# q, k and v products of an adaLN transformer block as split single passes, with q rows in three half sets and the work around them shifted

## The chip, the cores and the metric

The kernel runs on one core of a Trainium2 chip. The metric is the device time of one execution in microseconds (us), the median of several; the profile shows one execution of it. A second number, the span, is the time from the first to the last instruction of the profiled execution.

## The reference

For 32 batches of 512 tokens with 256 features, one transformer block with adaptive layer norm:

```python
mod = silu(c) @ wmod                       # per batch: sa, ca, ga, sb, cb, gb
h = layernorm(x) * (1 + ca) + sa
q, k, v = heads(h @ Wq + bq), heads(h @ Wk + bk), heads(h @ Wv + bv)   # 16 heads of 16
scores = (q / 4) @ k.T + 8 * position_bias[bucket(distance)]
x = x + ga * (softmax(scores) @ v @ Wo + bo)
h = layernorm(x) * (1 + cb) + sb
x = x + gb * fp4_linear(silu(fp4_linear(h, w_gate)) * fp4_linear(h, w_up), w_down)
```

`fp4_linear` rounds both operands, in blocks of 16, to a grid of FP4 values times a scale. The rounding makes the result sensitive to small errors ahead of it, which is why the kernel keeps its products near float32.

## The kernel before, in words

The program is written out for 36 iterations, n from -2 to 33, each of 16 slots s (0 to 15) of four places j (0 to 3). A place is written (s, j). Every engine walks through the same (s, j) in order, and semaphores tie them together; no scheduler moves anything. Three things run side by side in an iteration:

- **Attention of batch n.** In slot s the function `scores` writes two heads' scores for one block of 128 keys into a pair of PSUM banks, twice a slot (j = 0 and j = 2): a bf16 product over 121 rows (L630) and two or three small float16 products that add the band of the position bias (L633). ScalarE takes the exponential of each pair (L819); the pair's banks are free for the next `scores` only then. `weigh` at (s, 1) multiplies the probabilities of the slot before with the values (L665, float32).
- **Row maxima of the next batch.** At each (s, j) the function `maxima` (L647) makes one 128x512 tile of scores in one of two further banks, and VectorE (`reduce_max`, L1071 and L1073) adds the band and takes the maximum. The product of one place waits until the reduction of two places before has ended. The maxima of head h are made in slot h + 2. The jobs m0 and m1 turn the maxima of eight heads into rows that the scores product reads.
- **Jobs.** `job_table` gives each (s, j) zero or more jobs of TensorE, in three PSUM banks by turns: xT0, xT1 (transposes of normalised x), p0 to p3 (q and k products of batch n + 2, 256x256 times 256x512, a half of the heads each), v0 to v2 (v products), and the work on the token tiles, of which one tile per four slots passes through ctxT, wo, xqT, g0, g1, g2 (gate and up), oT, hT0, hT1 and down.

q and k are float32, and each is cut into three bf16 parts: ScalarE writes the product twice (`proj` in float32, part 0, L892), GpSimd subtracts part 0 (`rest`, L1287), ScalarE copies part 1 (L854), GpSimd subtracts again (`low`, L1294). The parts go to DRAM (L537), and `replicate` (L517) reads them back, six transfers for q and six for k of eight heads, into 96 rows of `q_rows` and `k_rows`, two buffers each of all 16 heads. The products p and v themselves are plain float32 matmuls of `h_t` (L704, L711), each of which the profile shows as two records. The products of the token tiles (`product`, L676) cut both operands into a high and a low float32r part instead and run three single passes: high times high, high times low, low times high.

In slots with s % 4 = 3 VectorE has the block scales of the hidden layer (L1108, L1110, L1112), on which GpSimd's multiply (L1357) waits, and on this ScalarE's square (L847) at (s, 3). At (s, 3) with s % 4 = 2 and (s, 0) after it VectorE subtracts the high part of the hidden transposes (`hq_l`, L1126), behind ScalarE's copies (L933, L936).

Iterations -2 and -1 hold only the start: setup of tables (`mod_and_bias_tables`, `spread_band`), the scales of the weights (`weight_scales`), q, k, v and maxima of batch 0.

Of the kernel before, what the change touches and what calls it, by code (L numbers as in the profile page):

```python
# [32 lines left out]
P = 128  # L33
# [9 lines left out]
HALF = 64  # L43
# [103 lines left out]
REST_AT, MID_AT, LOW_AT = (8, 9, 12, 13), ((8, 3), (9, 2), (12, 3), (13, 2)), (9, 10, 13, 14)  # L147
# [110 lines left out]
def build(nc, x, wq, wk, wv, wo, bq, bk, bv, bo, rel, wg, wu, wd, c_t, wmod, cst, rows_dram, band_dram, parts_dram, out):  # L258
    with ExitStack() as ctx:
# [7 lines left out]
        q_rows = [sb(f"q_rows{i}", [P, H, S], BF16) for i in range(2)]  # L267
# [4 lines left out]
        h_t = sb("h_t", [P, DT, S])  # L272
# [10 lines left out]
        w_q, w_k, w_v = (sb(n, [P, DT, D]) for n in ("w_q", "w_k", "w_v"))  # L283
# [8 lines left out]
        rev = sb("rev", [P, 3, P], F16)  # L292
# [5 lines left out]
        wait_pad = sb("wait_pad", [P, 1 + H * NT])  # L298
# [49 lines left out]
        a_act = Steps(sem("a_act"), "xh0 xh1 h0a h0b xh2 xh3 h1a h1b p0 hi0 p1 hi1 p2 hi2 p3 hi3")  # L348
# [42 lines left out]
        csb = flat(q_rows[1])  # L391
# [57 lines left out]
        def _(sp):  # L449
# [10 lines left out]
            for dst, src in ((w_q[:], wq), (w_k[:], wk), (w_v[:], wv)):  # L460
                load(dst, src.rearrange("(t p) n -> p t n", p=P), qkv_loaded)
# [9 lines left out]

            sp.wait_ge(su_act, SA["ind"])
            sp.dma_start(q_rows[0][CR], ind[CR].unsqueeze(1).broadcast_to([P - ROWS_QK, H, S])).then_inc(consts_placed, 16)
            sp.wait_ge(su_act, SA["band"])
            sp.dma_start(band_dram, band_sb).then_inc(band_stored, 16)
            sp.wait_ge(band_stored, 16)
            sp.wait_ge(su_pe, SP_["mod"])
            vec = band_dram
            for half in range(2):
                sp.dma_start(hank1[HALF * half:HALF * (half + 1)],  # L480
                             bass.AP(vec.tensor, vec.offset, [[1, HALF], [S, H], [1, 2 * P]])).then_inc(band_loaded, 16)
            sp.dma_start(hank2, bass.AP(vec.tensor, vec.offset,
                                        [[1, P], [S, H], [1, 3 * HALF]])).then_inc(band_loaded, 16)
# [24 lines left out]
            def replicate(it, half, back):  # L508

                n, par = it.n - back, (it.par + back) % 2  # L510

                wait(sp, scores_ready, 64 * n + 32 * (half + 1))
                for op, dst in ((0, q_rows[par]), (1, k_rows[par])):
                    wait(sp, parts_stored[2 * half + op], 16 * it.n + 16 * (3 - back))
                    src = parts_dram[par, half, op].rearrange("(h d) c n -> c d h n", d=HD)
                    for term, part in enumerate((TERMS_Q, TERMS_K)[op]):
                        sp.dma_start(dst[16 * term:16 * term + 16, 8 * half:8 * half + 8, :],  # L517
                                     src[part]).then_inc(replicated[half], 16)

            def emit(whole):  # L520
                it = whole
                n, par = it.n, it.par
                for s in range(16):
# [8 lines left out]
                    if s in (10, 14) and it.has(2):  # L532
                        for p in ((0, 1) if s == 10 else (2, 3)):
                            after(sp, low_pool, 4 * (n + 2) + p, "low")

                            wait(sp, replicated[p // 2], 16 * N_REP * (n + 1))
                            sp.dma_start(parts_dram[par, p // 2, p % 2], parts[:, p % 2]).then_inc(parts_stored[p], 16)  # L537
                    if s == 11 and it.has(2):
                        replicate(it, 0, 0)
# [29 lines left out]
        def _(pe):  # L569
# [23 lines left out]
            pe.wait_ge(qkv_loaded, 80)  # L593
# [806 lines left out]
```

## Time and profile before

| | before |
|---|---|
| runs | 3263.61, 3264.70, 3267.48 us; median 3264.7 |
| profiled execution | 3262.75 us, of which span 3260.9 us |
| busy, TensorE | 3137.3 us, 96% |
| busy, VectorE | 2765.6 us, 85% |
| busy, ScalarE | 2088.3 us, 64% |
| busy, GpSimd | 1732.0 us, 53% |
| mean granted TensorE clock | 0.982 of 2.4 GHz |

Busy times are unions of records. A matmul's record is longer than the time it holds the array, since the next starts before it ends; so the cost of a matmul is read from start to start. The same holds on VectorE and ScalarE, whose next instruction starts some 0.1 us before the end of the record in front.

### The profile page before, as it was taken

What the parts mean: (1) busy time and instruction counts of PE and PEld (TensorE: products, weight loads), DVE (VectorE), ACT (ScalarE), POOL (GpSimd) and SP (SyncE); (2) the same over time, 40 slices, a digit from 0 to 9 for tenths busy, and PEclk for the clock granted to TensorE, in tenths of its full rate; (3) what the DMA queues carried; (4) which work ended last, traced back from release to release, by engine and by line L of the source; (5) the groups of instructions that cost most, each with busy time, mean ns of one, the idle gap of its engine ahead of it and who ended that gap; (6) DMA issues with size and microseconds to landing.
All of it is one profiled execution on the core that took longest, in us unless ns stands there. A gap on an engine that the chain in (4) does not pass through costs nothing.

```text
span 3260.9 us, 67878 instructions
## 1 busy us (share of the span) xinstructions
PE 3137.3 (96%) x22404; PEld 1876.7 (58%) x22404; DVE 2765.6 (85%) x9960; ACT 2088.3 (64%) x3389; POOL 1732.0 (53%) x2104
## 2 busy tenths in 40 slices
PE   4899999999999999999999999999999999999985
PEld 1345566666656566665566665666666565666555
DVE  6678888888888888888888888888888888888865
ACT  2566666666666666666666666666666666666652
POOL 3415555555555555555555555555555555555455
PEclk7899999999999999999999999999999999999997
DMA  8344433334443324444233444332344433244000
GB/s 208 66 79 82 84 75 59 63 70 84 84 87 67 60 59 79 87 84 85 55 66 63 84 87 84 75 59 65 70 84 84 87 66 59 61 79 80 23 22 13
DMA packets 200187, 238.39 MB, mean 73 GB/s; under 512 B 23600, under 2 KB 178640, under 8 KB 199808
## 3 DMA queue, kind: packets, MB, share of 16 engines
q1 hardware_dynamic: 199840, 234.06, 37.1%
q8 instruction: 182, 2.98, 0.4%
q14 instruction: 165, 1.35, 0.2%
HBM read 164.57 MB, written 67.31 MB: 71 GB/s over the span
## 4 chain that ended last, share of the span: by engine, by line
PE 90%; issue 4%; DVE 3%; ACT 2%; DMA 1%; POOL 1%; SPq 0%; POOLq 0%; DVEq 0%; ACTq 0%
PE ps_x L676 25%; PE ps_o L665 15%; PE rings L647 14%; PE rings L630 14%; PE ps_x L704 6%; PE rings L633 5%; PE ps_x L711 3%; PE ps_x L722 2%; PE ps_x L743 2%; PE ps_x L735 1%; PE ps_x L728 1%; PE ps_x L697 1%; ACT probs L819 1%; DMA probs<-band_dram 0%; DVE row_max L1073 0%
## 5 line engine op out<-in xcount | busy, mean ns | idle before, releaser
L1073 DVE CUSTOM_DVE_ANT_0 rings<-rings,band_z 128x512 f32<-128x512 f32 x2048 | 1415.6, 696 | 70.5 <-issue 66.3
L819 ACT ACTIVATE probs<-rings 128x1024 f32<-128x1024 f32 x1024 | 1050.2, 1026 | 587.7 <-PE rings L633 587.5
L647 PE MATMUL rings<-k_rows,q_rows 120*128 120x512 bf16 x2048 | 790.6, 387 | 27.1 <-DVE row_max L1073 25.2
L630 PE MATMUL rings<-q_rows,k_rows 121*128 121x512 bf16 x2048 | 702.3, 383 | 12.3 <-ACT probs L819 11.2
L633 PEld LDWEIGHTS rings<-rev,band_t 128*128 128x128 f16 x5632 | 409.6, 98 | 299.9 <-issue 0.8
L665 PE MATMUL ps_o<-probs,values 128*32 128x512 f32 x4096 | 545.6, 605 | 0.0
L633 PE MATMUL rings<-rev,band_t 128*128 128x64 f16 x5632 | 500.6, 192 | 0.0
L647 PEld LDWEIGHTS rings<-k_rows,q_rows 120*128 120x128 bf16 x2048 | 197.4, 96 | 503.7 <-DVE row_max L1073 371.9
L1357 POOL TENSOR_TENSOR hidden<-hidden,inv 128x704 f32<-128x704 f32 x128 | 178.3, 1393 | 452.2 <-DVE inv L1112 452.2
L676 PE MATMUL ps_x<-w_gu_h,xq_h 128*128 128x512 f32 (+1 forms) x768 | 356.9, 465 | 1.1 <-DVE xq_l L1118 1.1
L1172 DVE SCALAR_TENSOR_TENSOR tanh<-tanh,ps_x 128x256 f32<-128x256 f32 (+1 forms) x384 | 152.3, 397 | 169.6 <-ACT tanh L929 165.3
L1073 DVE DVE_READ_ACCUMULATOR2_ANT row_max<- 128x1 f32 x2048 | 289.1, 141 | 0.0
L676 PE MATMUL ps_x<-w_gu_h,xq_l 128*128 128x512 f32 (+1 forms) x768 | 289.0, 376 | 0.0
L676 PE MATMUL ps_x<-w_gu_l,xq_h 128*128 128x512 f32 (+1 forms) x768 | 285.7, 372 | 0.0
L676 PE MATMUL ps_x<-w_dn_h,hq_h 128*128 128x256 f32 x768 | 240.6, 313 | 18.2 <-DVE hq_l L1126 18.2
L630 PEld LDWEIGHTS rings<-q_rows,k_rows 121*128 121x128 bf16 x2048 | 198.5, 97 | 92.7 <-issue 42.0
L1351 POOL TENSOR_TENSOR ffn_in<-ffn_in,inv 128x256 f32<-128x256 f32 x128 | 79.4, 620 | 303.8 <-DVE inv L1112 303.8
L1328 POOL TENSOR_TENSOR hidden<-hidden,magic 128x704 f32<-128x704 f32 x128 | 200.1, 1563 | 39.4 <-ACT magic L850 38.3
L676 PE MATMUL ps_x<-w_dn_l,hq_h 128*128 128x256 f32 x768 | 219.0, 285 | 0.0
L676 PE MATMUL ps_x<-w_dn_h,hq_l 128*128 128x256 f32 x768 | 218.7, 285 | 0.0
L1287 POOL TENSOR_TENSOR proj<-proj,parts 128x512 f32<-128x512 f32 x128 | 163.7, 1279 | 88.9 <-ACT parts L892 88.9
L1330 POOL TENSOR_TENSOR hidden<-hidden,magic 128x704 f32<-128x704 f32 x128 | 197.5, 1543 | 10.0
(180 smaller groups left out, 6330.4 us busy)
## 6 DMA issues: line engine op xcount, KB each, us to landing
parts_dram<-parts SPq DMA_DIRECT2D x128, 384.0 KB, 2.6
q_rows<-parts_dram SPq DMA_DIRECT2D x384, 128.0 KB, 5.4
k_rows<-parts_dram SPq DMA_DIRECT2D x384, 128.0 KB, 7.9
mod_rows<-mod_rows_dram SPq DMA_DIRECT2D x32, 640.0 KB, 10.0
x_in<-in_x SPq DMA_DIRECT2D x32, 512.0 KB, 5.3
x_mid<-in_x SPq DMA_DIRECT2D x128, 128.0 KB, 2.0
out<-x_mid SPq DMA_DIRECT2D x128, 128.0 KB, 2.2
k_rows<-band_dram SPq DMA_DIRECT2D x2, 1024.0 KB, 9.5
```

The costliest lines, as they stand in the source:

```text
L630: mm(ps_s[:, bank, :], kr[0:ROW_MAX + 1, h, k0:k0 + P], qr[0:ROW_MAX + 1, h, :], start=True, stop=False)
L633: m = mm(ps_s[:, bank, k0 + w * HALF:k0 + (w + 1) * HALF], band_t[:, h, P - w * HALF:2 * P - w * HALF], rev[:, 0, 0:HALF], start=False, st ...
L647: mm(ps_m[:, bank, :], q_rows[par][0:ROW_MAX, h, j * P:(j + 1) * P], k_rows[par][0:ROW_MAX, h, :], start=True, stop=True).then_inc(mscores ...
L665: m = mm(ps_o[32 * j:32 * j + 32, :], values[:, par, kb, h * VW:h * VW + 32], prob(u, j), start=kb == 0, stop=kb == NT - 1)
L676: m = mm(out, left[a][:, dt, :], right[b][:, dt, columns], start=i == 0, stop=i == len(terms) - 1)
L704: m = mm(ps[:, :], w[:, dt, half * P:(half + 1) * P], h_t[:, dt, :], start=dt == 0, stop=dt == DT - 1)
L819: A(prob_pair(s, j), ps_s, ACT.Exp).then_inc(exp_done, 1)
L1073: v.tensor_tensor_reduce(ps, ps, band_z[:, bias:bias + S], 1.0, LOWEST, ALU.add, ALU.max, row_max[:, par, 4 * h + j:4 * h + j + 1]).then_i ...
L1287: q.tensor_tensor(pr, pr, parts[:, p % 2, 0, :], ALU.subtract).then_inc(rest_pool.sem, 1)
L1328: q.tensor_tensor(hid, hid, magic3[:], ALU.add).then_inc(f3_pool.sem, 1)
L1330: q.tensor_tensor(hid, hid, magic3[:], ALU.subtract).then_inc(f3_pool.sem, 1)
L1357: q.tensor_tensor(blocks(hid), blocks(hid), spread(inv3[:], FF // BLK), ALU.mult).then_inc(f2_pool.sem, 1)
```

## The change

- **Products.** The weights wq, wk, wv are cut once into a high and a low float32r part (`w_qkv_h` by ScalarE, `w_qkv_l` by GpSimd). ScalarE writes the transposed, scaled x twice, exact (over `x_in`) and high (`h_h`), four activations of 128x256 per half in place of two; GpSimd subtracts (`h_l`, slots 6 and 7). p and v jobs become `product` with three passes.
- **q rows.** `q_rows` (two buffers of 16 heads) becomes `q_half` (three buffers of 8 heads), used by turns. The copy of heads 0 to 7 of the next batch is issued at slot 0, that of heads 8 to 15 at slot 8, and parts are stored one by one at slots 11, 13, 15 and 0.
- **Shifts.** Maxima of head h are made in slot h + 4. The jobs move: m1 from (2, 2) to (4, 1), m0 from (10, 2) to (12, 1), p0 from (7, 0) to (8, 2), p1 from (8, 2) to (10, 2), p2 from (11, 0) to (12, 2), p3 from (12, 2) to (14, 2). `rest` runs in slots 9, 11, 13, 15 (before 8, 9, 12, 13), part 1's copy at (9, 2), (11, 2), (13, 2), (15, 2), `low` in slots 10, 12, 14, 15 (before 9, 10, 13, 14).
- **Setup.** The band goes through DRAM as two float16 parts, so that it is loaded as float16 and the casts of three large tables fall away; the last step of the band's table comes behind `weight_scales`.
- **Maxima.** The one-element write in front of each of the 2048 reductions (L1071) is dropped; the reduction itself waits.

The diff, cut to what is spoken of:

```diff
-    batch = {(0, 2): "v0", (2, 2): "m1", (3, 0): "v1", (4, 2): "v2", (5, 1): "xT0", (6, 2): "xT1", (7, 0): "p0",
-             (8, 2): "p1", (10, 2): "m0", (11, 0): "p2", (12, 2): "p3"}
+    batch = {(0, 2): "v0", (4, 1): "m1", (3, 0): "v1", (4, 2): "v2", (5, 1): "xT0", (6, 2): "xT1", (8, 2): "p0",
+             (10, 2): "p1", (12, 1): "m0", (12, 2): "p2", (14, 2): "p3"}
...
-REST_AT, MID_AT, LOW_AT = (8, 9, 12, 13), ((8, 3), (9, 2), (12, 3), (13, 2)), (9, 10, 13, 14)
+REST_AT, MID_AT, LOW_AT = (9, 11, 13, 15), ((9, 2), (11, 2), (13, 2), (15, 2)), (10, 12, 14, 15)
+MAX_LAG = 4
...
-        q_rows = [sb(f"q_rows{i}", [P, H, S], BF16) for i in range(2)]
+        q_half = [sb(f"q_half{i}", [P, H // 2, S], BF16) for i in range(3)]
...
+            def replicate(b, half):
+
+                used = 64 * (b - 2) + 64 if half == 0 else 64 * (b - 1) + 32
+                wait(sp, scores_ready, used)
+                for op in range(2):
+                    wait(sp, parts_stored[2 * half + op], 16 * (b + 1))
+                    dst = q_half[(2 * b + half) % 3] if op == 0 else k_rows[b % 2][:, 8 * half:8 * half + 8, :]
...
-                shift, h = (1, s - 2) if s >= 2 else (0, s + 14)
+                shift, h = (1, s - MAX_LAG) if s >= MAX_LAG else (0, s + 16 - MAX_LAG)
...
-                    w, half = (w_q, w_k)[p % 2], p // 2
-                    after(pe, a_act, n + 2, "h1b")
-                    for dt in range(DT):
-                        m = mm(ps[:, :], w[:, dt, half * P:(half + 1) * P], h_t[:, dt, :],
-                               start=dt == 0, stop=dt == DT - 1)
+                    half = p // 2
+                    after(pe, h_pool, n + 2, "lo1")
+                    cut = [w[:, p % 2, :, half * P:(half + 1) * P] for w in (w_qkv_h, w_qkv_l)]
+                    m = product(ps[:, :], cut, (h_h, h_l))
...
-                                for dt in range(DT):
-                                    i = A(h_t[:, dt, 2 * half * P:(2 * half + 2) * P].rearrange("p (k q) -> p k q", k=2),
+                                for o in (h_exact(half), h_cols(h_h, half)):
+                                    for dt in range(DT):
+                                        A(o[:, dt, :].rearrange("p (k q) -> p k q", k=2),
                                           src[:, :, dt, :], ACT.Identity, scale=mod_col[:, dt:dt + 1],
                                           bias=mod_col[:, 2 + dt:3 + dt]).then_inc(a_act.sem, 1)
...
-                dve.wait_ge(band_loaded, 48)
-                step(v.tensor_copy(hank2_half, hank2))
-                mark("hank")
-                step(v.tensor_copy(band_t[:], hank1))
-                step(v.tensor_tensor(band_t[HALF:P], hank1[HALF:P], band_t[HALF:P], ALU.subtract))
+
+            def band_table():
+
...
-                v.memset(wait_pad[:, 1 + 4 * h + j:2 + 4 * h + j], 0.0)
...
                     mod_and_bias_tables()
                     weight_scales()
+                    band_table()
...
+                    if s in (6, 7) and it.has(2):
+                        half = s - 6
+                        after(pool, a_act, n + 2, f"h{half}b")
+                        q.tensor_tensor(h_cols(h_l, half), h_exact(half), h_cols(h_h, half).bitcast(F32),
+                                        ALU.subtract).then_inc(h_pool.sem, 1)
```

How the instructions stand at three places. TensorE, from xT1 at (6, 2) to `weigh` of slot 7, before (transposes of x and of hidden, one maxima, the scores pair of (7, 0), a maxima, p0, `weigh`):

```order
L697 MATMUL ps_x<-ident,x_in 128x128 x4
L743 MATMUL ps_x<-ident,hidden 128x128 x4
L647 MATMUL rings<-k_rows,q_rows 128x512
L746 MATMUL ps_x<-ident,hidden 128x128
L747 MATMUL ps_x<-ident,hidden 128x128
L630 MATMUL rings<-q_rows,k_rows 128x512
L633 MATMUL rings<-rev,band_t 128x64 x2
L630 MATMUL rings<-q_rows,k_rows 128x512
L633 MATMUL rings<-rev,band_t 128x64 x2
L647 MATMUL rings<-k_rows,q_rows 128x512
L704 MATMUL ps_x<-h_t,w_q 128x512 x2
L665 MATMUL ps_o<-probs,values 32x512 x4
```

The same place in the changed program:

```order
L722 MATMUL ps_x<-ident,x_in 128x128 x4
L766 MATMUL ps_x<-ident,hidden 128x128 x4
L672 MATMUL rings<-k_rows,q_half 128x512
L769 MATMUL ps_x<-ident,hidden 128x128
L770 MATMUL ps_x<-ident,hidden 128x128
L655 MATMUL rings<-q_half,k_rows 128x512
L658 MATMUL rings<-rev,band_t 128x64 x2
L655 MATMUL rings<-q_half,k_rows 128x512
L658 MATMUL rings<-rev,band_t 128x64 x2
L672 MATMUL rings<-k_rows,q_half 128x512
L690 MATMUL ps_o<-probs,values 32x512 x4
```

The q product between the maxima of (7, 0) and `weigh` is gone from here; nothing takes its place. ScalarE, from the exponential of (6, 2) to that of (7, 0), before:

```order
L819 ACTIVATE probs<-rings 128x1024
L882 ACTIVATE h_t<-ps_x,mod_col 128x256 x2
L933 ACTIVATE hq_h<-ps_x 128x512
L842 ACTIVATE magic<-ffn_in 128x256
L936 ACTIVATE hq_h<-ps_x 128x256
```

and in the changed program:

```order
L844 ACTIVATE probs<-rings 128x1024
L908 ACTIVATE x_in<-ps_x,mod_col 128x256 x2
L908 ACTIVATE h_h<-ps_x,mod_col 128x256 x2
L959 ACTIVATE hq_h<-ps_x 128x512
L867 ACTIVATE magic<-ffn_in 128x256
L962 ACTIVATE hq_h<-ps_x 128x256
```

Two more activations stand ahead of `hq_h`. GpSimd, from the scaling of ffn_in in slot 14 to slot 0 (parts: `low`; proj: `rest`; hidden, inv: the multiply that ScalarE's square waits for), before:

```order
L1351 TENSOR_TENSOR ffn_in<-ffn_in,inv 128x256
L1294 TENSOR_TENSOR parts<-proj,parts 128x512
L1357 TENSOR_TENSOR hidden<-hidden,inv 128x704
L1361 TENSOR_TENSOR ffn_in<-ffn_in,scale 128x256
L1323 TENSOR_TENSOR x_mid<-x_mid,mod_rows 128x256
```

and in the changed program:

```order
L1385 TENSOR_TENSOR ffn_in<-ffn_in,inv 128x256
L1323 TENSOR_TENSOR parts<-proj,parts 128x512
L1316 TENSOR_TENSOR proj<-proj,parts 128x512
L1323 TENSOR_TENSOR parts<-proj,parts 128x512
L1391 TENSOR_TENSOR hidden<-hidden,inv 128x704
L1395 TENSOR_TENSOR ffn_in<-ffn_in,scale 128x256
L1357 TENSOR_TENSOR x_mid<-x_mid,mod_rows 128x256
```

`rest` and `low` of p3 now stand in slot 15, directly ahead of the multiply of hidden, and this `low` waits for ScalarE's copy at (15, 2).

## Rows read from the trace of the kernel before

**Rows 1.** Busy by window: us, PE, PEld, DVE, ACT, POOL (count), clock, DMA share, GB/s.

```profile
300.00:3000.00 2700.00, 2699.30 (x19648) 1631.98 (x19646) 2372.70 (x8701) 1813.94 (x2953) 1480.67 (x1828) 1.00 0.39 74
```

**Rows 2.** Timeline of TensorE: start, us, engine, line; a p job, then float32r passes.

```profile
1614.64 1.88 PE L704 MATMUL ps_x<-h_t,w_k 128*128 128x512 f32 x4
1616.35 0.38 PE L647 MATMUL rings<-k_rows,q_rows 120*128 120x512 bf16 x1
...
1618.35 0.39 PE L676 MATMUL ps_x<-w_gu_l,xq_h 128*128 128x512 f32 x1
...
1619.28 0.40 PE L676 MATMUL ps_x<-w_gu_h,xq_l 128*128 128x512 f32 x1
```

**Rows 3.** Timeline of TensorE: scores (6, 2), p0, weigh 7, scores (8, 0).

```profile
1577.26 0.38 PE L630 MATMUL rings<-q_rows,k_rows 121*128 121x512 bf16 x1
...
1580.19 1.92 PE L704 MATMUL ps_x<-h_t,w_q 128*128 128x512 f32 x4
1582.04 1.07 PE L665 MATMUL ps_o<-probs,values 128*32 128x512 f32 x8
...
1586.39 0.38 PE L630 MATMUL rings<-q_rows,k_rows 121*128 121x512 bf16 x1
```

**Rows 4.** Timeline of ScalarE, from the exponential of (6, 2) to that of (7, 0).

```profile
1578.08 1.03 ACT L819 ACTIVATE probs<-rings 128x1024 f32<-128x1024 f32 x1 [1.55 <-PE rings L633]
1579.00 1.01 ACT L882 ACTIVATE h_t<-ps_x,mod_col 128x256 f32<-128x256 f32 x2
1579.89 0.60 ACT L933 ACTIVATE hq_h<-ps_x 128x512 fp32r<-128x512 f32 x1
...
1580.94 1.05 ACT L819 ACTIVATE probs<-rings 128x1024 f32<-128x1024 f32 x1
```

**Rows 5.** Timeline of VectorE, from (6, 3) to (7, 1), writes and accumulator reads left out.

```profile
1580.60 0.69 DVE L1126 TENSOR_TENSOR hq_l<-ps_x,hq_h 128x512 fp32r<-128x512 f32 x1 [0.81 <-ACT hq_h L933]
1581.21 0.69 DVE L1073 CUSTOM_DVE_ANT_0 rings<-rings,band_z 128x512 f32<-128x512 f32 x1
...
1581.83 0.42 DVE L1126 TENSOR_TENSOR hq_l<-ps_x,hq_h 128x256 fp32r<-128x256 f32 x1
1582.17 0.69 DVE L1073 CUSTOM_DVE_ANT_0 rings<-rings,band_z 128x512 f32<-128x512 f32 x1
...
1582.78 0.88 DVE L1108 TENSOR_REDUCE scale<-hidden 128x44 f32<-128x704 f32 x1
...
1584.27 0.70 DVE L1073 CUSTOM_DVE_ANT_0 rings<-rings,band_z 128x512 f32<-128x512 f32 x1
```

**Rows 6.** Page, costliest groups: the write in front of each reduction.

```profile
L1071 DVE MEMSET wait_pad<- 128x1 f32 x2048 | 120.8, 59 | 1.0 <-PE rings L647 0.9
```

**Rows 7.** Timelines of POOL, ACT and PE at the end of slot 15.

```profile
1533.30 1.16 POOL L1294 TENSOR_TENSOR parts<-proj,parts 128x512 bf16<-128x512 f32 x1
1537.08 1.39 POOL L1357 TENSOR_TENSOR hidden<-hidden,inv 128x704 f32<-128x704 f32 x1 [2.62 <-DVE inv L1112]
...
1535.79 1.03 ACT L819 ACTIVATE probs<-rings 128x1024 f32<-128x1024 f32 x1 [0.82 <-PE rings L633]
1538.50 0.79 ACT L847 ACTIVATE magic<-hidden 128x704 bf16<-128x704 f32 x1 [1.68 <-POOL hidden L1357]
...
1540.80 0.38 PE L630 MATMUL rings<-q_rows,k_rows 121*128 121x512 bf16 x1
```

**Rows 8.** Timelines of the start: VectorE's casts and first reduction, TensorE's first scores.

```profile
43.78 1.76 DVE L1006 CAST w_setup<-probs 128x3072 f16<-128x3072 f32 x1 [8.69 <-DMA probs<-band_dram]
...
52.36 4.70 DVE L1015 CAST band_z<-rings 128x384 f16<-128x384 f32 x8
...
71.28 0.69 DVE L1073 CUSTOM_DVE_ANT_0 rings<-rings,band_z 128x512 f32<-128x512 f32 x1
...
128.94 0.63 PE L630 MATMUL rings<-q_rows,k_rows 121*128 121x512 bf16 x1
```

**Rows 9.** Page, DMA issues: KB each, us from issue to landing.

```profile
k_rows<-parts_dram SPq DMA_DIRECT2D x384, 128.0 KB, 7.9
```

More of the change, by code:

```diff
@@ L430, in prob_pair, with q_of, h_exact, h_cols @@
             return probs[:, at:at + 2, :]
+        def q_of(b, h):
+            return q_half[(2 * b + h // 8) % 3][:, h % 8, :]
+        def h_exact(half):
+            return x_in[:, 2 * half:2 * half + 2, :].rearrange("p k d -> p (k d)").rearrange("p (t q) -> p t q", t=DT)
+        def h_cols(h, half):
+            return h[:, :, 2 * half * P:(2 * half + 2) * P]
         def gate_up(w, kt, op, n0):
@@ L459, in _ @@
             load(b_k[:], bk, qkv_loaded)
-            for dst, src in ((w_q[:], wq), (w_k[:], wk), (w_v[:], wv)):
-                load(dst, src.rearrange("(t p) n -> p t n", p=P), qkv_loaded)
+            for i, src in enumerate((wq, wk, wv)):
+                load(w_qkv_raw[:, DT * D * i:DT * D * (i + 1)].rearrange("p (t n) -> p t n", t=DT),
+                     src.rearrange("(t p) n -> p t n", p=P), qkv_loaded)
             load(bo_sb, bo.partition_broadcast(B), bias_loaded)
@@ L506, in load_rows, with store_parts @@
                              .rearrange("p b n -> p (b n)")).then_inc(rows_loaded[par], 16)
[L508 to L515, printed above, removed]
-                    for term, part in enumerate((TERMS_Q, TERMS_K)[op]):
-                        sp.dma_start(dst[16 * term:16 * term + 16, 8 * half:8 * half + 8, :],
-                                     src[part]).then_inc(replicated[half], 16)
+            def replicate(b, half):
[4 more added lines that the diff above has]
+                    dst = q_half[(2 * b + half) % 3] if op == 0 else k_rows[b % 2][:, 8 * half:8 * half + 8, :]
+                    src = parts_dram[b % 2, half, op].rearrange("(h d) c n -> c d h n", d=HD)
+                    for term, part in enumerate((TERMS_Q, TERMS_K)[op]):
+                        sp.dma_start(dst[16 * term:16 * term + 16], src[part]).then_inc(replicated[half], 16)
+            def store_parts(b, p):
+                after(sp, low_pool, 4 * b + p, "low")
+                wait(sp, replicated[p // 2], 16 * N_REP * (b - 1))
+                sp.dma_start(parts_dram[b % 2, p // 2, p % 2], parts[:, p % 2]).then_inc(parts_stored[p], 16)
             def emit(whole):
@@ L531, in emit @@
                                      ).then_inc(xres_loaded[t], 16)
[L532 to L539, printed above, removed]
+                    if s in (11, 13, 15) and it.has(2):
+                        store_parts(n + 2, (11, 13, 15).index(s))
+                    if s == 13 and n == FIRST:
+                        replicate(0, 0)
                     if s == 0 and it.has(2) and (it.steady or n > FIRST + 1):
@@ L542, in emit @@
                     if s == 0 and it.has(1):
-                        replicate(it, 1, 1)
+                        if n > FIRST + 1:
+                            replicate(n + 1, 0)
+                        store_parts(n + 1, 3)
                     if s == 0 and not it.steady and n == FIRST + 1:
                         place_consts()
+                    if s == 8 and it.has(1) and n > FIRST:
+                        replicate(n + 1, 1)
                     if s == 8 and not it.steady and n == FIRST:
@@ L627, in scores @@
                     wait(pe, exp_done, it.n * 32 + 2 * s + j // 2)
-                qr, kr = q_rows[it.par], k_rows[it.par]
+                qr, kr = q_of(it.n, h), k_rows[it.par]
                 k0 = kb * P
-                mm(ps_s[:, bank, :], kr[0:ROW_MAX + 1, h, k0:k0 + P], qr[0:ROW_MAX + 1, h, :], start=True, stop=False)
+                mm(ps_s[:, bank, :], kr[0:ROW_MAX + 1, h, k0:k0 + P], qr[0:ROW_MAX + 1, :], start=True, stop=False)
                 windows = 3 if kb < NT - 1 else 2
@@ L977, in mod_and_bias_tables @@
                 dve.wait_ge(su_act, SA["rel"])
-                for i in range(3):
-                    step(v.tensor_copy(rev[:, i, :], csb[:, C_JLO + P * i:C_JLO + P * (i + 1)]))
+                step(v.tensor_tensor(band_lo, setup_b[0:H, 0, :], band_hi, ALU.subtract))
+                mark("lo")
+                for i, at in enumerate((C_JLO, C_J2)):
+                    step(v.tensor_copy(rev[:, i, :], csb[:, at:at + P]))
                 step(v.tensor_tensor(kc[0][CR], over_u(c0[CR]), over_h(csb[CR, C_M:C_M + NU]), ALU.mult))
```

94 lines of the change are left out of this document (52 added, 42 removed).

## The prediction

> **What bounds the kernel now.** I read the busy table by windows first. Between 300 and 3000 us TensorE is busy in 2699.3 of 2700 us at full granted clock, VectorE in 2372.7 (88%), ScalarE in 1813.9, GpSimd in 1480.7 [rows 1]. So TensorE's instruction stream is the time, and a us taken out of it is a us won, as long as nothing else arrives late. Since its records overlap, small waits hide in that 100%; I found them in its timeline, from start to start. VectorE at 88%, with the two-bank ring between `maxima` and `reduce_max`, is the next bound. The slots with s % 4 = 3 are where it is close: there it has the block scales, and what covers it on TensorE is a p or v job.
>
> **Part 1, the products, on the path.** A p job is four records of 512 columns and takes 1.71 us to the next start (1614.64 to 1616.35). The float32r passes of gate and up stand 0.93 / 4 = 0.2325 us apart (1618.35 to 1619.28) [rows 2]. Six of them are 1.395 us, so a p job gains 0.315 us, the four of a batch 1.26 us. The v products have half the columns of the p products (4 x 2 x 256 against 4 x 2 x 512), and by the same two prices gain 0.63 us. That is 1.89 us a batch, for some 30 batches **57 us**. The weights must be loaded six times in place of four records' loads, but the passes of gate and up do that too and their spacing holds it.
>
> **Part 2, slot 7 loses its cover.** Before, p0 lies between the scores of (7, 0) and `weigh` (1580.19 to 1582.04), and slot 8 begins at 1586.39 [rows 3]. Without p0 TensorE would be there 1.7 us earlier. Follow what else must be done, with the same clock. Slot 5's two extra activations make the exponential of (5, 2), and with it TensorE, late by 0.2 us: scores (6, 2) start at 1577.5 and their exponential at 1578.25. Two activations are worth 0.89 us (1579.00 to 1579.89), so the four of xT1 last from 1579.15 to 1580.95, where before `hq_h` started at 1579.89 [rows 4]. `hq_h` ends at 1581.55. VectorE's `hq_l` takes 0.61 us, the reduction of (6, 3) 0.62, the second `hq_l` 0.34, the next reduction 0.61 and the block scales 1.49 (1582.78 to 1584.27) [rows 5]. So the reduction of (6, 3) ends at 1582.8, that of (7, 0) at 1583.75, that of (7, 1) at 1585.85. TensorE's maxima of (7, 1), which needs the first, would be ready at 1581.9 and starts at 1582.85; the scores of (7, 2), 0.2 us later, find the exponential of (7, 0) just done; maxima (7, 2) go at 1583.8; `down`, 2.1 us, ends at 1586.15. Slot 8 begins at 1586.4: nothing is won from moving p0 away, **1.7 us a batch is lost as waiting**.
>
> **Part 3, p1 and p3 ahead of hT0.** In slots 10 and 14 the job itself covers 1.4 us of TensorE, but its two activations (1.15 us) stand before `hq_h` on ScalarE, and VectorE's `hq_l` and slot 11 or 15 come later by as much. The same chain as in part 2 gives 0.65 us of waiting in slot 11, where the timeline of before has 0.3, and 0.65 in slot 15, where it has 0.5. **0.5 us a batch.**
>
> **Part 4, GpSimd in slot 15.** Before, GpSimd's last `low` started at 1533.30, long ahead of hidden's multiply at 1537.08. Now it waits for ScalarE's copy at (15, 2). Count from X, the start of the exponential of (15, 2), 1535.79 before. ScalarE is free at X + 0.92, the copy is done at X + 1.54, `low` (1.16) at X + 2.75, the multiply (1.39) at X + 4.15; the square (0.7 to the next start) lets the exponential of (0, 0) begin at X + 4.9 and end at X + 5.9. Scores (0, 2) wait for that; before, they started at X + 5.0 (1540.80) [rows 7]. Part 3's 0.15 us is already in TensorE's time, so 0.75 us is waited there. Behind the square stand the `magic` copy and `ctx_h`, on which VectorE waits for `ctx_l` before it can reduce (0, 1): the maxima of (0, 3) lose another 0.6 us. **1.35 us a batch.** wo comes after and waits for nothing more.
>
> The waits come to 3.55 us a batch, over some 29 iterations with p jobs and tiles **+103 us**. GpSimd's own 2 x 1.2 us a batch, at 55% busy, end in slot 7 long before p0 at (8, 2): nothing. m0 and m1 only change place: nothing. If the two `h_l` collide with VectorE, some tenths of a us move; I take nothing.
>
> **Part 5, the write.** It is 59 ns, 2048 times, 120.8 us of VectorE's busy time [rows 6], 3.8 us a batch. But a reduction with its write and accumulator read takes 0.61 to 0.62 us to the next start, no more than the plain `hq_l` of 512 elements, 0.61 (1580.60 to 1581.21) [rows 5]. So the write lies inside the start of its reduction. Bounds: 0 and 59 ns; I take 0, by that row.
>
> **Part 6, transfers.** The copy of heads 8 to 15 starts when the scores of slot 7 are done, and is needed at (12, 0), four slots or 24 us later. Twelve issues take 5.8 us and land 7.9 us after issue [rows 9]: 14 us. Heads 0 to 7 start as soon as p2's store is out, in slot 15, and have longer. Nothing waits.
>
> **Part 7, the start.** VectorE waits 8.7 us for the band and casts until 52.36, does the band's last step, the weights' scales, and reduces first at 71.28; the first scores of batch 0 start at 128.94 [rows 8]. Now the band falls out of VectorE's way (43.78 less 8.69, i.e. 35.1, to 52.36: 17 us), and it could begin at 54. TensorE's first maxima then waits for its rows, which the longer chain of h and parts brings at about 56, so 15 us are won. Before the first scores stand 48 maxima in place of 56 (0.65 us each: 5 us), and four p jobs at the low clock are 1 us shorter each. Together **-24 us**; the eight maxima come back at the end, where slots 2 and 3 of iteration 31 now have them: **+2 us**. Lower bound of the gain: 8 us, if the later maxima are held by the activations of the weights; upper: 32.
>
> **Sum.** -57 + 103 - 24 + 2 = +24 us on the profiled 3262.75 us: 3287. That execution is 2 us below the median of its runs (3264.7), so I say **3288 us**. By the waits' errors (a third of 103) and the start's bounds this case lies between 3260 and 3320.
>
> **Rivals.**
> - *The slack takes it all* (faster). The chains of parts 2 to 4 are put together from rows of a program in which they don't stand so; if VectorE and ScalarE run ahead after each wait, the waits do not appear: 3264.7 - 57 - 22 = 3186 us. For it: 12% of VectorE's time is idle. Against: each chain starts from an instruction that cannot run ahead, the transposes or the exponential of the same slot. Chance 0.12. Half of the waits give 3236 us: 0.16.
> - *The write was worth its 59 ns.* Then three reductions in each chain of parts 2 and 3 and one in part 4 come 0.06 us earlier, 0.6 us a batch, 17 us: 3271. Chance 0.12. The page "VectorE: DVE Perf Modes" of the Trainium skill (Rules for kernel authors) says that waiting time between Vector instructions can't be fused away and that one should minimise the number of instructions; by that rule this rival is right. Rows 5 speak against it.
> - *The transfers come late* (slower still). If landing takes over 18 us under load, the maxima of (12, 0) wait, and TensorE with them; 5 us a batch would give 3430 us. It decides only from 10 us above the landing of rows 9: 0.04.
> - *The start is not shortened*, because ScalarE's weight activations hold it: 3304. Chance 0.1.
>
> The forecast itself has 0.46.
>
> **Chances and range.** A measurement of this kernel tells some 0.2% (6.5 us) from no change. Faster by more: both parts of the first rival and the low tail of the forecast and of the second, 0.12 + 0.16 + 0.05 = 0.33. Within: 0.09, around the write's 3271 and the forecast's lower end. Slower: 0.58. The range leaves out the rival without any wait and the late transfers: 3203 to 3325. The forecast's own is 3260 to 3320.
>
> **What would show it.** In the timeline of TensorE p jobs of 1.4 us; in slot 7 a maxima that starts right behind the reduction of (6, 3); in slot 0 scores (0, 2) that start right behind an exponential, with ScalarE's square before it released by GpSimd; a first scores near 105 us; reductions still 0.61 us apart. The idle time put down to row_max and probs on TensorE should grow by some 100 us together. If TensorE still runs from start to start without gaps in slots 7 and 0, parts 2 and 4 are wrong and the kernel is faster.

## The result, and the profile after

The changed kernel takes **3335.8 us** (median, 3335.08 to 3336.43) against 3266.1 for the kernel before in the same session: ratio **1.0218**, 95% interval 1.0205 to 1.0231. It is 70 us slower where I had forecast 23 us slower; the sign was right, and the time lies 11 us above the upper end of the range. Of the profiled executions, after spans 3333.2 us and before 3260.9.

Busy table by window of after, 300 to 3000 us, the columns of [rows 1]:

```profile
300.00:3000.00 2700.00, 2586.13 (x19425) 1626.64 (x19421) 2302.57 (x6662) 1795.55 (x2969) 1511.04 (x1824) 1.00 0.36 71
```

TensorE, busy in 2699.3 us of this window before, now stands idle in 114, at the same full granted clock. No other engine took its place: VectorE and ScalarE are less busy in the window too, and GpSimd is busy in 56% of it. So the time went into waiting, not into work. The page says for what (the columns are busy us, mean ns, idle us before and its releaser; the line number of `reduce_max` is 1098 now):

```profile
L672 PE MATMUL rings<-k_rows,q_half 120*128 120x512 bf16 x2048 | 790.3, 387 | 124.8 <-DVE row_max L1098 124.2
L655 PE MATMUL rings<-q_half,k_rows 121*128 121x512 bf16 x2048 | 702.0, 383 | 18.9 <-ACT probs L844 15.9
L872 ACT ACTIVATE magic<-hidden 128x704 bf16<-128x704 f32 x128 | 101.2, 791 | 220.6 <-POOL hidden L1391 220.6
L1151 DVE TENSOR_TENSOR hq_l<-ps_x,hq_h 128x512 fp32r<-128x512 f32 (+1 forms) x256 | 141.1, 553 | 165.3 <-ACT hq_h L959 158.8
```

and of before:

```profile
L647 PE MATMUL rings<-k_rows,q_rows 120*128 120x512 bf16 x2048 | 790.6, 387 | 27.1 <-DVE row_max L1073 25.2
L630 PE MATMUL rings<-q_rows,k_rows 121*128 121x512 bf16 x2048 | 702.3, 383 | 12.3 <-ACT probs L819 11.2
L1126 DVE TENSOR_TENSOR hq_l<-ps_x,hq_h 128x512 fp32r<-128x512 f32 (+1 forms) x256 | 141.1, 553 | 49.1 <-ACT hq_h L933 42.4 <-ACT hq_h L936 4.9
L847 ACT ACTIVATE magic<-hidden 128x704 bf16<-128x704 f32 x128 | 101.2, 791 | 126.1 <-POOL hidden L1357 126.1
```

Maxima wait 97.7 us more in all, scores 6.6: the "some 100 us together" that the prediction asked for. VectorE waits 116 us more for `hq_h`, and ScalarE's square 94 more for GpSimd's multiply: the two late starters that parts 2 to 4 named. These gaps between records are only a part of the waiting, since records overlap; the table below counts it from start to start.

**Where, slot by slot.** I took from TensorE's timeline, for 8 batches between 1200 and 2000 us, the start of each slot's `weigh` and the medians of their distances. "Work" is what the change moves or shortens on TensorE by the prices of part 1 (a transpose of m0 or m1 is 0.11, 1633.84 to 1633.95 in the trace of after); what is left of the difference is waiting.

| slots | before | after | difference | work | waiting | waiting forecast |
|---|---|---|---|---|---|---|
| 0 | 6.41 | 7.92 | +1.51 | -0.16 (v0) | 1.67 | 1.35 |
| 2 to 4 | 17.65 | 17.33 | -0.32 | -0.47 (v1, v2) | 0.15 | 0 |
| 5 | 6.53 | 6.75 | +0.22 | 0 | 0.22 | 0 |
| 6, 7 | 11.50 | 11.56 | +0.06 | -1.71 (p0) | 1.77 | 1.7 |
| 8 | 7.25 | 6.95 | -0.30 | -0.31 | 0.01 | 0 |
| 10, 11 | 11.31 | 11.60 | +0.29 | -0.43 (p, m0) | 0.72 | 0.35 |
| 12 | 7.25 | 7.23 | -0.02 | -0.20 (p, m0) | 0.18 | 0 |
| 14, 15 | 9.76 | 11.59 | +1.83 | +1.40 (p3) | 0.43 | 0.15 |
| all | 95.94 | 99.20 | +3.26 | -1.88 | 5.15 | 3.55 |

Slots 1, 9 and 13 did not change. The medians hide that some batches grew by 3.6 us: the 28 full iterations grew by 93.0 us together, and the two ahead of them, which hold less work, by 6.3. The start gives 28 back: the first scores of batch 0 come at 100.53 us, before at 128.94 [rows 8].

```profile
58.61 0.70 DVE L1098 CUSTOM_DVE_ANT_0 rings<-rings,band_z 128x512 f32<-128x512 f32 x1 [3.31 <-PE rings L672]
...
100.53 0.38 PE L655 MATMUL rings<-q_half,k_rows 121*128 121x512 bf16 x1
```

**Slot 7**, timelines of ScalarE, VectorE and TensorE of after; they answer to [rows 3 to 5]:

```profile
1598.46 1.03 ACT L844 ACTIVATE probs<-rings 128x1024 f32<-128x1024 f32 x1 [1.20 <-PE rings L658]
1599.38 1.01 ACT L908 ACTIVATE x_in<-ps_x,mod_col 128x256 f32<-128x256 f32 x2
1600.28 1.03 ACT L908 ACTIVATE h_h<-ps_x,mod_col 128x256 fp32r<-128x256 f32 x2
1601.18 0.62 ACT L959 ACTIVATE hq_h<-ps_x 128x512 fp32r<-128x512 f32 x1
...
1601.90 0.69 DVE L1151 TENSOR_TENSOR hq_l<-ps_x,hq_h 128x512 fp32r<-128x512 f32 x1 [1.45 <-ACT hq_h L959]
1602.51 0.69 DVE L1098 CUSTOM_DVE_ANT_0 rings<-rings,band_z 128x512 f32<-128x512 f32 x1
...
1600.83 1.06 PE L690 MATMUL ps_o<-probs,values 128*32 128x512 f32 x8
1603.31 0.39 PE L672 MATMUL rings<-k_rows,q_half 120*128 120x512 bf16 x1 [1.42 <-DVE row_max L1098]
```

This is part 2's chain, link by link: four activations, then `hq_h`, `hq_l`, the reduction of (6, 3), and the maxima of (7, 1). VectorE's next instruction starts at 1603.11, and the maxima 0.2 us later; they had waited 1.42 us since the end of `weigh`'s record.

### The profile page after: what moved, and what is told of

Same layout as the page of the kernel before. It is cut to its first block, busy times and chain, and to the rows that moved or that the text cites. A ratio compares the mean times of both kernels' runs of the same rounds, so it can differ in the third digit from the quotient of the medians.

```text
span 3333.2 us, 67047 instructions
## 1 busy us (share of the span) xinstructions
PE 3104.5 (93%) x22916; PEld 1940.1 (58%) x22916; DVE 2766.3 (83%) x7909; ACT 2138.1 (64%) x3518; POOL 1824.8 (55%) x2169
## 4 chain that ended last, share of the span: by engine, by line
PE 73%; issue 9%; ACT 8%; DVE 6%; POOL 4%; DMA 0%; DVEq 0%; ACTq 0%; POOLq 0%; SPq 0%
PE ps_x L701 30%; PE rings L672 12%; PE ps_o L690 11%; PE rings L655 11%; PE rings L658 4%; ACT h_h L908 2%; POOL hidden L1391 2%; DVE hq_l L1151 2%; ACT probs L844 2%; ACT hq_h L959 1%; DVE rings L1098 1%; PE ps_x L745 1%; ACT x_in L908 1%; POOL parts L1323 1%; PE ps_x L751 1%
## 5 line engine op out<-in xcount | busy, mean ns | idle before, releaser
L672 PE MATMUL rings<-k_rows,q_half 120*128 120x512 bf16 x2048 | 790.3, 387 | 124.8 <-DVE row_max L1098 124.2
L655 PE MATMUL rings<-q_half,k_rows 121*128 121x512 bf16 x2048 | 702.0, 383 | 18.9 <-ACT probs L844 15.9
L672 PEld LDWEIGHTS rings<-k_rows,q_half 120*128 120x128 bf16 x2048 | 196.7, 96 | 612.7 <-DVE row_max L1098 525.3
L1151 DVE TENSOR_TENSOR hq_l<-ps_x,hq_h 128x512 fp32r<-128x512 f32 (+1 forms) x256 | 141.1, 553 | 165.3 <-ACT hq_h L959 158.8
L655 PEld LDWEIGHTS rings<-q_half,k_rows 121*128 121x128 bf16 x2048 | 198.3, 97 | 94.3 <-ACT probs L844 54.9
L872 ACT ACTIVATE magic<-hidden 128x704 bf16<-128x704 f32 x128 | 101.2, 791 | 220.6 <-POOL hidden L1391 220.6
L1362 POOL TENSOR_TENSOR hidden<-hidden,magic 128x704 f32<-128x704 f32 x128 | 201.0, 1570 | 61.3 <-ACT magic L875 60.7
```

What stands on the lines that cost most here:

```text
L655: mm(ps_s[:, bank, :], kr[0:ROW_MAX + 1, h, k0:k0 + P], qr[0:ROW_MAX + 1, :], start=True, stop=False)
L672: mm(ps_m[:, bank, :], q_of(b, h)[0:ROW_MAX, j * P:(j + 1) * P], k_rows[par][0:ROW_MAX, h, :], start=True, stop=True).then_inc(mscores_rea ...
L872: A(magic3[:], hidden[:, g % 2, :], ACT.Square, scale=ROOT).then_inc(f3_act.sem, 1)
L1151: v.tensor_tensor(hq_l[:, k0:k1, :].rearrange("p a q -> p (a q)"), ps[:, 0:(k1 - k0) * P], hq_h[:, k0:k1, :].rearrange("p a q -> p (a q)") ...
L1362: q.tensor_tensor(hid, hid, magic3[:], ALU.add).then_inc(f3_pool.sem, 1)
```

## The experiments

All ten ran beside the kernel before; each ratio is to that, with its 95% interval, and each slot length is measured as in the table above.

**1. The write alone**, from the kernel before:

```diff
-                v.memset(wait_pad[:, 1 + 4 * h + j:2 + 4 * h + j], 0.0)
```

> The kernel before, with nothing changed but the one-element write in front of each reduction taken out. Theory (the write lies inside the start of its reduction): the same time as before, 3266 us within 4 us, while VectorE's busy time falls by some 120 us; reductions stay 0.61 us apart. Rival (each write holds VectorE for its 59 ns): at least 17 us faster, 3249 or less, up to 121 us where VectorE's chain sets the pace.

3262.8 us, ratio 0.9989 (0.9980 to 0.9998): 3 to 4 us won by the medians, 0.7 to 6.5 by the interval. Groups of VectorE's instructions between 300 and 3000 us, first of before, then of this run:

```profile
L1073 DVE CUSTOM_DVE_ANT_0 rings<-rings,band_z 128x512 f32<-128x512 f32 x1802 | 1247.1, 696 | 23.1 <-issue 21.0
L1071 DVE MEMSET wait_pad<- 128x1 f32 x1802 | 106.3, 59 | 0.0
```

```profile
L1072 DVE CUSTOM_DVE_ANT_0 rings<-rings,band_z 128x512 f32<-128x512 f32 x1804 | 1237.5, 690 | 23.6 <-PE rings L647 17.3
```

The write's 59 ns vanish and the reduction is 6 ns shorter. The small gain alone proves nothing, since VectorE does not bind here. The records do: in the trace of before the write starts some 0.02 us behind the start of its reduction and ends inside it,

```profile
1533.87 0.70 DVE L1073 CUSTOM_DVE_ANT_0 rings<-rings,band_z 128x512 f32<-128x512 f32 x1
1533.89 0.06 DVE L1071 MEMSET wait_pad<- 128x1 f32 x1
```

and from a reduction's start to its accumulator read it is 0.611 us with the write and 0.607 without. For the same reason the busy time of VectorE, a union of records, fell by 19 us only (2765.6 to 2746.3), where I had expected 120.

**2. The write, put back into the changed kernel**, where VectorE's chains are exposed (into four cells in turn):

```diff
+                v.memset(wait_pad[:, 1 + j:2 + j], 0.0)
```

> The changed kernel with the one-element write in front of each reduction put back (into one of four cells in turn). Here VectorE's chains in slots 7, 11, 15 and 0 are on the path, where the kernel before had cover. Theory (the write lies inside its reduction's start): 3336 us within 4 us. Rival (each write holds VectorE for its 59 ns): 0.6 us a batch, 17 us: 3353 us or more.

3340.5 us, ratio 1.0226 (1.0209 to 1.0243), the changed kernel's being 1.0218. The two intervals overlap; by the medians it is 4.6 us, the same few as in the first run, just outside the 4 that I had allowed, and far from 17. The slots sum to 99.32 us against 99.20. The rival falls; if the write is worth anything it is 2 ns apiece.

**3. GpSimd's low of p3 behind the multiplies of slot 15:**

```diff
+                    if s < 15:
                         low(it, s)
                     if r == 3 and it.has_tile(s, 1):
...
+                    if s == 15:
+                        low(it, s)
```

> The changed kernel, with one step moved: in slot 15 GpSimd's last subtraction for p3 (low) stands behind its two multiplies in place of ahead of them. Theory (part 4: slot 0 waits for the multiply that low holds up, and the multiply collides with VectorE's scalar_tensor_tensor): slot 0, 1.5 us longer than before, gives back 1.3 to 1.7 us a batch, 38 to 48 us; 3288 to 3298 us, and no scalar_tensor_tensor of 1.5 us is left. Rival (the lost time belongs to the shift by four heads and the half sets): under 10 us, 3326 or more.

3291.8 us, ratio 1.0079 (1.0062 to 1.0096): 45 us back. Slot 0 is 6.41 us, as before the change; the other fifteen read the same to 0.01 us. TensorE in slot 0, of the changed kernel and of this run:

```profile
1558.33 1.06 PE L690 MATMUL ps_o<-probs,values 128*32 128x512 f32 x8
1559.96 0.39 PE L672 MATMUL rings<-k_rows,q_half 120*128 120x512 bf16 x1 [0.56 <-DVE row_max L1098]
...
1560.74 0.39 PE L655 MATMUL rings<-q_half,k_rows 121*128 121x512 bf16 x1 [0.17 <-ACT probs L844]
...
1562.98 0.39 PE L672 MATMUL rings<-k_rows,q_half 120*128 120x512 bf16 x1 [0.53 <-DVE row_max L1098]
```

```profile
1540.01 1.06 PE L690 MATMUL ps_o<-probs,values 128*32 128x512 f32 x8
1541.01 0.39 PE L672 MATMUL rings<-k_rows,q_half 120*128 120x512 bf16 x1
...
1541.46 0.38 PE L655 MATMUL rings<-q_half,k_rows 121*128 121x512 bf16 x1
...
1543.14 0.39 PE L672 MATMUL rings<-k_rows,q_half 120*128 120x512 bf16 x1
```

From `weigh` the scores (0, 2) stand at 2.41 us in one and 1.45 in the other, the maxima (0, 3) at 4.65 and 3.13. So the scores lost 0.96 us, the maxima 0.56 more: part 4's two terms (0.75 and 0.6), together 1.5. One step of 1.16 us on an engine that is busy 56% of the time cost 45 us of span.

**4. xT1 behind `hq_h`,** at the start of slot 7 where p0 was, GpSimd's second `h_l` at the slot's end:

```diff
-    batch = {(0, 2): "v0", (4, 1): "m1", (3, 0): "v1", (4, 2): "v2", (5, 1): "xT0", (6, 2): "xT1", (8, 2): "p0",
+    batch = {(0, 2): "v0", (4, 1): "m1", (3, 0): "v1", (4, 2): "v2", (5, 1): "xT0", (7, 0): "xT1", (8, 2): "p0",
```

> The changed kernel, with xT1 moved from the middle of slot 6 to the start of slot 7, where p0 stood before, so that its four activations come behind hq_h on ScalarE; GpSimd's second h_l goes to the end of slot 7. Theory (part 2: VectorE comes late into slot 7 because hq_h comes late, and nothing covers it on TensorE): slots 6 and 7 together, 11.56 us now, fall by 1.2 to 1.7 us; 35 to 50 us in all, 3286 to 3301 us. Rival (the same reductions and block scales bound slot 7 wherever hq_h stands): under 10 us.

3303.8 us, ratio 1.0112 (1.0097 to 1.0127): 35 us back. Slots 6 and 7 take 4.85 + 5.50 = 10.35 us in place of 11.56, 1.21 us less; that is the lower end of what was expected, and the time lies 3 us outside it. Without any waiting they would take 11.50 less p0's 1.71, 9.79 us; 0.56 us stay, in slot 6.

**5. p1 and p3 behind `hq_h`,** at (11, 0) and (15, 0), where before p2 stood in the first and nothing in the second:

```diff
-             (10, 2): "p1", (12, 1): "m0", (12, 2): "p2", (14, 2): "p3"}
+             (11, 0): "p1", (12, 1): "m0", (12, 2): "p2", (15, 0): "p3"}
-REST_AT, MID_AT, LOW_AT = (9, 11, 13, 15), ((9, 2), (11, 2), (13, 2), (15, 2)), (10, 12, 14, 15)
+REST_AT, MID_AT, LOW_AT = (9, 12, 13, 0), ((9, 2), (12, 2), (13, 2), (0, 2)), (10, 13, 14, 1)
```

with the stores of p1 and p3 in slots 14 and 2 of SP.

> The changed kernel, with p1 moved from (10, 2) to (11, 0) and p3 from (14, 2) to (15, 0), behind the copies of hidden's transposes on ScalarE; their rest, mid and low follow one to two slots later, those of p3 in slots 0 and 1 of the next iteration. xT1 and p0 stay. Theory (parts 3 and 4): slots 10 and 11 give back 0.5 us, 14 and 15 0.4, slot 0 1.3 to 1.7, less what ScalarE's two activations in slot 15 now delay; 50 to 70 us, 3266 to 3286 us. Rival (transfers or the shift hold the kernel): no gain, or slower, since the copy of heads 8 to 15 has less time.

3243.8 us, ratio 0.9930 (0.9915 to 0.9945): 94 us back, more than expected, and already below the kernel before. Slot 0 is 6.26 us (1.66 less), 10 and 11 together 10.94 (0.66 less), 12 7.08 (0.15 less), 14 and 15 10.94 (0.65 less); 3.1 us a batch. I had priced the moves by the waiting that I took from the table (0.5 and 0.4), but the table shows only what was added to the waits that the kernel before already had in these slots. From start to start the changed kernel waits 0.89 us in slots 10 and 11, and as much in 14 and 15; here some 0.24 us of each is left. The groups of the whole run, listed by line:

```profile
L673 PE MATMUL rings<-k_rows,q_half 120*128 120x512 bf16 x2048 | 790.1, 387 | 53.6 <-DVE row_max L1099 51.8 <-DMA k_rows<-parts_dram 0.9
L1152 DVE TENSOR_TENSOR hq_l<-ps_x,hq_h 128x512 fp32r<-128x512 f32 (+1 forms) x256 | 141.2, 553 | 60.1 <-ACT hq_h L960 52.5 <-ACT hq_h L963 4.9 <-issue 1.0
```

It is the release by `hq_h` that shrank, from 158.8 us to 52.5. The shift of the maxima by four heads and the three half sets are still in this kernel, and heads 8 to 15 have less time for their way through DRAM; the wait for `k_rows` is 0.9 us in the whole run. The rivals that blame transfers or the shift fall.

**6. The products, undone:**

```diff
-                    m = product(ps[:, :], cut, (h_h, h_l))
+                    for dt in range(DT):
+                        m = mm(ps[:, :], cut[0][:, dt, :].bitcast(F32), h_h[:, dt, :].bitcast(F32), start=dt == 0, stop=dt == DT - 1)
```

and the v job alike.

> The changed kernel, with the p and v products as plain float32 matmuls of the high parts alone (the low parts are left out of the products, so q, k and v lose precision); everything else, the activations and GpSimd's h_l too, stays. Theory (part 1: TensorE's stream is the time, a p job costs 0.315 us more, the v jobs of a batch 0.63): 57 us slower where all of it is on the path, 40 where slot 0's waiting swallows v0 and slots 10 and 14 swallow some; 3376 to 3393 us. Rival (products hide beside the waits of VectorE): under 15 us.

3386.3 us, ratio 1.0378 (1.0362 to 1.0393): 52 us slower than the changed kernel. By slots: 0.30 to 0.33 us for each p job, 0.30 for v1, 0.13 for v2, and nothing for v0, which the wait in slot 0 swallows. Part 1's prices were right; that v0's would count was not.

**7. The copy to `h_h` by GpSimd,** so that ScalarE has two activations for each xT:

```diff
-                                for o in (h_exact(half), h_cols(h_h, half)):
+                                for o in (h_exact(half),):
...
+                        q.tensor_copy(h_cols(h_h, half), h_exact(half)).then_inc(h_pool.sem, 1)
```

> The changed kernel, with ScalarE writing only the exact h (two activations for each xT, as before) and GpSimd copying it to h_h ahead of its subtraction. Theory (part 2: half of slot 7's loss is ScalarE's two more activations ahead of hq_h, and slot 5's 0.2 us too): slot 5 falls by 0.2 us, slots 6 and 7 by 0.9, together 1.1 us a batch, 32 us: 3304 us; GpSimd's two copies are 2.4 us a batch beside work with room. Rival (only cover on TensorE decides, ScalarE's activations hide): under 5 us. Second rival (GpSimd is then late in slot 7, as it was in slot 15, and slot 8 waits): slower than the changed kernel by up to 1 us a batch.

3302.4 us, ratio 1.0120 (1.0103 to 1.0137): 32 us back. Slot 5 is 0.22 us shorter, slot 6 0.17, slot 7 0.75. So the two extra activations alone make slot 5's loss and half of slot 7's, and the maxima of slot 7 still wait, for 0.67 us in place of 1.42:

```profile
1581.48 0.39 PE L672 MATMUL rings<-k_rows,q_half 120*128 120x512 bf16 x1 [0.67 <-DVE row_max L1098]
```

The other half can be read by comparing with the kernel before. There, too, two activations stood ahead of `hq_h`, and slots 6 and 7 had no waiting; here they take 4.24 + 6.40 = 10.64 us, 0.85 more than the 9.79 without waiting. So p0's place covered 0.85 us, not all of the 1.7. No run puts another job into that place in the changed kernel, so this is a comparison of two kernels that differ in more. Experiment 4 shows that cover is not the only cure: with all four activations behind `hq_h` the maxima of slot 7 start without a wait.

**8. The start: the band's eight steps ahead of the weights' scales:**

```diff
                     mod_and_bias_tables()
-                    weight_scales()
                     band_table()
+                    weight_scales()
```

> The changed kernel, with the band's eight steps on VectorE in the setup ahead of the weights' scales, as before, in place of behind them. Theory (part 7: the start is shorter because 17 us of waiting and casting left VectorE, and what is left is VectorE's work in a row, 37 to 54 us, in either order): 3336 us within 4 us, the first scores at 98 to 104 us. Rival (the gain is the order: the scales cover the band's way through DRAM): first scores up to 12 us later, 3348 us.

3337.4 us, ratio 1.0214 (1.0198 to 1.0229), no change. The first reduction comes at 61.13 us in place of 58.61, the first scores at 103.90 in place of 100.53: the order is worth some 3 us of the 28 at the first scores, though nothing of it shows in the time, and the rest is work and waiting that left VectorE.

**9. Both moves together** (experiments 4 and 5 in one kernel):

> The changed kernel with both moves that gave something by themselves: xT1 at the start of slot 7, p1 and p3 at the starts of slots 11 and 15 with their rest, mid and low behind, low of p3 in slot 1. Theory (each wait is local to its slots, so the gains add: 32 us for xT1's place, 92 us for p1's and p3's): 3208 to 3215 us, 1.6% below the kernel before. Rival (VectorE at over 85% becomes the bound once the waits are gone): 3235 or more.

3208.2 us, ratio **0.9831** (0.9817 to 0.9846). The gains add: 126 us by the ratios, 35 and 94 one by one. VectorE is busier in the window than in the kernel before, 2393.9 us against 2372.7, and does not bind.

**10. The moves, and the copy by GpSimd:**

> All moves as in the run before the last, and the copy to h_h by GpSimd. Theory: slot 5's 0.2 us comes off as well, and 0.1 to 0.3 us in slots 6 to 8, 10 us under that run: 3200 us. Rival (GpSimd's last h_l comes too late for p0 in slot 8 or holds hidden's chain): 5 to 30 us slower than that run.

3194.5 us, ratio **0.9789** (0.9774 to 0.9803): 2.1% below the kernel before and 4.2% below the changed one, the best of the study, and 14 us below experiment 9 where I had expected 10. A batch takes 94.46 us. Slot 8 is longer by 0.15 us: its p0 now starts just behind GpSimd's last `h_l`. Window 300 to 3000 us, and the maxima's group:

```profile
300.00:3000.00 2700.00, 2695.86 (x20411) 1695.47 (x20407) 2391.72 (x7001) 1846.31 (x2986) 1597.32 (x1957) 1.00 0.38 74
```

```profile
L673 PE MATMUL rings<-k_rows,q_half 120*128 120x512 bf16 x2048 | 791.7, 387 | 14.5 <-DVE row_max L1099 11.4 <-DMA k_rows<-parts_dram 2.0
```

TensorE is again busy from end to end, the maxima wait less than before the change, and now the shorter products and the shorter start show in the time: 94.46 us a batch is 1.48 below 95.94, some 44 us, and the first scores, at 103.67 us, come 25 earlier; the measured gain is 68.

## Why the prediction was right in sign and wrong in size

- *Part 1 (products, -57 us):* right as a price. Taken out of the stream by themselves they cost 52 us. But v0's 0.16 us a batch stands ahead of maxima that wait in any case (part 4), and the sum counted it as won.
- *Part 2 (slot 7, 1.7 us):* right at 1.77, and half of it, the two extra activations, is shown by experiment 7. But I used slot 5's lateness of 0.2 us as the start of the chain and did not charge it: it is 0.22 us a batch of its own.
- *Part 3 (p1 and p3, 0.5 us):* **this step was mis-sized**; the slots lost 0.72 and 0.43 us, 1.15 in place of 0.5. The mechanism is there, but I forecast 0.65 us of waiting in each pair of slots, and it is 0.89. TensorE of the changed kernel in slot 11:

```profile
1626.22 1.07 PE L690 MATMUL ps_o<-probs,values 128*32 128x512 f32 x8
1627.95 0.39 PE L672 MATMUL rings<-k_rows,q_half 120*128 120x512 bf16 x1 [0.66 <-DVE row_max L1098]
...
1628.67 0.22 PE L658 MATMUL rings<-rev,band_t 128*128 128x64 f16 x2
1628.89 0.39 PE L672 MATMUL rings<-k_rows,q_half 120*128 120x512 bf16 x1
```

  From `weigh` to the first maxima it is 1.73 us, in slot 11 of before 1.00: 0.73 of waiting. From the small product to the second maxima it is 0.22 in place of 0.06: another 0.16, which my chain left out. It is the same in slot 15. And I set these waits against waits of before that I read as 0.3 and 0.5 us; the medians of eight batches are 0.16 and 0.43. The 0.3 came from the one full batch of before that took 96.10 us where the others took 95.93. The first error is 0.48 us a batch, the second 0.2.
- *Part 4 (slot 0, 1.35 us):* the mechanism right, the size 0.3 short in the table's count. GpSimd's multiply took 1.57 us where the row of before has 1.39 [rows 7], and the 0.16 us of v0 is waited away here.
- *Left out:* slot 12 lost 0.18 us and slots 2 to 4 lost 0.15, for which the prediction had nothing. No experiment was made for these; experiment 5 gave 0.15 of slot 12 back.
- *Part 5 (the write, 0):* right within 2 ns of 59. The Trainium skill, page "VectorE: DVE Perf Modes" (Rules for kernel authors), by which fewer instructions mean less waiting between them, would have given 17 us or more here. Experiments 1 and 2 measured some 4 by the medians: for an instruction of one element in front of a long one, the measurement decides against the rule.
- *Part 6 (transfers):* nothing waits, right. *Part 7 (start, -24):* -28; the first reduction came 12.7 us earlier where I said 15, and the stretch from there to the first scores was shortened by 15.7 where I said 9, so two errors partly cancelled. The +2 at the end is 1.1: slots 2 to 4 of iteration 31 take 15.66 us, before 14.58.

So the waits were 5.15 us a batch in place of 3.55: 29.5 times 1.6 is 47 us, the 48 that the forecast of 3288 fell short. Part 3 has 0.65 of the 1.6, part 4 0.32, slot 5 0.22, slot 12 0.18, slots 2 to 4 0.15, slot 7 0.07. The first rival, that slack takes the waits, is refuted by TensorE's rows in slots 7, 11, 15 and 0. The range failed because I gave the waits' error as a third, and they were 45% larger. The chains held what the longest path needs and left out a second wait behind the first and slots that looked untouched; nearly all of these errors point the same way.

## What to carry to other kernels

When a tuned stream is cut by 57 us, first look at what the removed or moved pieces covered: here moving a job of 1.71 us won nothing, since 0.85 us of VectorE's chain came to light behind it and two more activations ahead of that chain took another 0.92. Place work by whom it stands ahead of on each engine's queue, not by busy shares: placing the same jobs behind `hq_h`, and GpSimd's `low` behind its multiply, gave back 126 us (experiment 9), and two copies handed to GpSimd another 14 (experiment 10). Price a chain's errors on one side, read the waits of before from several batches, and compare slot by slot, since local waits add and each can be given back by itself.

## What the runs showed of the hardware that I had not expected

Once in each batch a VectorE instruction of 0.42 us took 1.50. Timelines of GpSimd and VectorE of the changed kernel:

```profile
1655.48 1.16 POOL L1323 TENSOR_TENSOR parts<-proj,parts 128x512 bf16<-128x512 f32 x1 [3.36 <-ACT parts L879]
1656.60 1.57 POOL L1391 TENSOR_TENSOR hidden<-hidden,inv 128x704 f32<-128x704 f32 x1
...
1656.34 0.58 DVE L1185 SCALAR_TENSOR_TENSOR ffn_in<-magic,ffn_in 128x256 f32<-128x256 bf16 x1
1656.96 1.50 DVE L1187 SCALAR_TENSOR_TENSOR ffn_in<-magic,ffn_in 128x256 f32<-128x256 bf16 x1
1658.38 0.69 DVE L1098 CUSTOM_DVE_ANT_0 rings<-rings,band_z 128x512 f32<-128x512 f32 x1
```

The late `low` pushed GpSimd's multiply onto the scalar_tensor_tensor, which reads two operands from SBUF and ends 0.3 us behind it. The multiply itself takes 1.57 us here and 1.39 in slots 3, 7 and 11. The scalar_tensor_tensor's mean over the steady part is 690 ns; with `low` behind the multiplies (experiment 3) it is 425 again:

```profile
L1187 DVE SCALAR_TENSOR_TENSOR ffn_in<-magic,ffn_in 128x256 f32<-128x256 bf16 x109 | 75.2, 690 | 3.7
```

```profile
L1187 DVE SCALAR_TENSOR_TENSOR ffn_in<-magic,ffn_in 128x256 f32<-128x256 bf16 x110 | 46.8, 425 | 3.8
```

The Trainium skill, page "SBUF — State Buffer" (Who interferes with whom), says that a VectorE instruction with two SBUF inputs contends with a GpSimd instruction that reads SBUF; this trace agrees. How much of slot 0's loss is the collision's and how much is the late multiply's no run separates, since one move removed both. The rows let it be estimated. Counted from the start of `weigh` (1657.54), the multiply starts 0.94 us ahead, in experiment 3 2.28 ahead (1537.73 and 1540.01): 1.34 us later. With 0.18 us of its own lengthening that is 1.52, all that slot 0 lost. VectorE's long instruction adds nothing to it by this reading: the scores behind it wait for the exponential, and VectorE itself then stands idle for `ctx_h`, both behind ScalarE's square.

```profile
1658.20 0.79 ACT L872 ACTIVATE magic<-hidden 128x704 bf16<-128x704 f32 x1 [2.80 <-POOL hidden L1391]
1658.90 1.01 ACT L844 ACTIVATE probs<-rings 128x1024 f32<-128x1024 f32 x1
...
1659.96 0.39 PE L655 MATMUL rings<-q_half,k_rows 121*128 121x512 bf16 x1 [0.17 <-ACT probs L844]
...
1661.05 0.42 DVE L1143 TENSOR_TENSOR ctx_l<-ps_x,ctx_h 128x256 fp32r<-128x256 f32 x1 [0.99 <-ACT ctx_h L937]
```
